# Two matmul stages in a fixed order: the second stage of batch 0 moved ahead of batch 1's products

## What is computed

```python
x = x + matmul(fake_quant(layernorm(x)), fake_quant(ctx))       # per batch
x = x + ffn(layernorm(x))
# fake_quant(v) = (clip(round(v / s + z), 0, 255) - z) * s
# ffn(y): logits = y @ W_router.T                               # 8 experts
#         combine = top 2 of softmax(logits), renormalised
#         h = (y @ A_e.T) * combine_e                           # rank 16 each
#         out = y @ W_base.T + b_base + 2.0 * sum_e(h_e @ B_e.T)
```

## Time and profile before

| | before |
|---|---|
| median of the runs | 189.27 us |
| span of the profiled execution | 187.8 us |
| TensorE (PE) busy | 164.8 us, 88% |
| VectorE (DVE) busy | 127.8 us, 68% |
| ScalarE (ACT) busy | 75.0 us, 40% |
| GpSimd (POOL) busy | 37.8 us, 20% |
| HBM read, written | 18.38 MB, 4.19 MB |

### The profile page before, as it was taken

How to read it: one execution, slowest core, us unless ns; L and a number is a source line. 1 busy time by engine, 2 the same in 40 slices (tenths; PEclk the granted TensorE clock), 3 DMA queues, 4 the chain that set the end, 5 groups by cost and what they waited for, 6 DMA issues and landing times.

```text
span 187.8 us, 2573 instructions
## 1 busy us (share of the span) xinstructions
PE 164.8 (88%) x946; PEld 88.2 (47%) x946; DVE 127.8 (68%) x284; ACT 75.0 (40%) x100; POOL 37.8 (20%) x110
## 2 busy tenths in 40 slices
PE   6639997894697969369999999999999999999992
PEld 3323443351263427126556556556556556556541
DVE  6996577899666995995872872872882882831821
ACT  3476393997285923545124124124124124120000
POOL 8804504045500000080031031031021021000000
PEclk9975999999789999999999999999999999999999
DMA  5999999999300000000200200200200200200211
GB/s 116 401 417 410 409 408 407 409 409 411 127 5 0 0 0 0 0 0 3 112 2 3 112 0 0 112 3 0 112 0 3 112 0 0 108 7 0 105 65 56
DMA packets 6780, 22.74 MB, mean 121 GB/s; under 512 B 880, under 2 KB 1136, under 8 KB 6768
## 3 DMA queue, kind: packets, MB, share of 16 engines
q1 hardware_dynamic: 6624, 22.58, 30.8%
q10 hardware_dynamic: 144, 0.00, 0.0%
HBM read 18.38 MB, written 4.19 MB: 120 GB/s over the span
## 4 chain that ended last, share of the span: by engine, by line
PE 66%; DVE 28%; issue 3%; POOL 1%; DVEq 0%; POOLq 0%
PE ps L753 39%; PE ps L713 8%; PE ps L743 6%; DVE w_lo L522 4%; PE ps L722 3%; DVE xs L468 3%; PE ps L735 2%; PE ps L734 2%; PE ps L736 2%; DVE a L595 2%; DVE xs L417 2%; DVE a L454 2%; DVE bnx L427 2%; DVE bnx L425 2%; DVE a_t L461 1%
## 5 line engine op out<-in xcount | busy, mean ns | idle before, releaser
L753 PE MATMUL ps<-w_hi,yt_hi 128*128 128x512 f16 x128 | 39.5, 380 | 6.0 <-DVE w_lo L522 6.0
L713 PE MATMUL ps<-a,a_t 128*128 128x512 f16 x128 | 34.6, 407 | 6.9 <-DVE a_t L461 6.8
L753 PE MATMUL ps<-w_hi,yt_lo 128*128 128x512 f16 x128 | 39.4, 379 | 0.0
L753 PE MATMUL ps<-w_lo,yt_hi 128*128 128x512 f16 x128 | 39.4, 379 | 0.0
L287 ACT ACTIVATE a<-stage,prm,inv_s 128x1024 uint8<-128x1024 f32 x16 | 19.6, 1240 | 12.0 <-DMA stage<-in_ctx_kv 11.7
L713 PEld LDWEIGHTS ps<-a,a_t 128*128 128x128 f16 x128 | 12.4, 103 | 23.6 <-DVE a_t L461 10.2
L550 DVE MAX8 top<-ps 128x8 f32<-128x8 f32 x8 | 1.4, 175 | 30.6 <-PE ps L736 30.6
L235 POOL TENSOR_SCALAR root<-mvy 128x1 f32<-128x1 f32 (+1 forms) x7 | 2.9, 413 | 87.9 <-DVE mvy L421 87.9
L337 ACT ACTIVATE y<-xs,y_bias,y_scale 128x1024 f32<-128x1024 f32 x8 | 9.9, 1239 | 26.5 <-POOL y_bias L258 26.4
L753 PEld LDWEIGHTS ps<-w_hi,yt_hi 128*128 128x128 f16 x128 | 11.4, 98 | 18.3 <-DVE w_lo L522 7.7
L753 PEld LDWEIGHTS ps<-w_hi,yt_lo 128*128 128x128 f16 x128 | 12.5, 98 | 15.1
(11 more groups left out here) (127 smaller groups left out, 266.7 us busy)
## 6 DMA issues: line engine op xcount, KB each, us to landing
stage<-in_ctx_kv SPq DMA_DIRECT2D x16, 512.0 KB, 13.5
stage<-in_w_t SPq DMA_DIRECT2D x8, 512.0 KB, 11.8
xs<-in_x SPq DMA_DIRECT2D x7, 512.0 KB, 13.5
out_dram<-xs SPq DMA_DIRECT2D x7, 512.0 KB, 2.7
ar_raw<-in_ar_t SPq DMA_DIRECT2D x1, 544.0 KB, 15.9
xs<-in_x SPq DMA_DIRECT2D x2, 256.0 KB, 3.7
b_raw<-in_b_t SPq DMA_DIRECT2D x1, 512.0 KB, 11.2
bias_sb<-in_bias SPq DMA_DIRECT2D x1, 512.0 KB, 12.0
```

The costliest lines, as they stand in the source:

```text
L713: last = nc.tensor.matmul(ps[:, s1_bank(t) + h, :], a1_t[:, t % 4, k, :], a2[:, n, h * H:(h + 1) * H], start=k == 0, stop=k == K - 1)
L753: ins = nc.tensor.matmul(ps[:, OUT_BANK[p] + h, :], part, rhs[:, k, h * H:(h + 1) * H], start=k == 0 and part is hi and rhs is w_hi, stop= ...
```

## The change

Line numbers in `order` rows are those of the kernel that the rows are of.

- **SyncE** loads ar and w straight behind batch 0's context, then tile 4 of x, b, the bias and the other x tiles. Batch 1's context comes last and takes over the slots of w, so each of its tiles waits for a w_lo.
- **TensorE** runs the first stage of tiles 0 to 3 alone. Then come the wide products of tiles 0 and 1 in two passes: the parts hi x hi and lo x hi (which need only w_hi) first, w_lo's part later, with narrow, lora and the column sums of batch 1 in between. The products of tiles 4 to 7 stand inside the wide products of tiles 2 to 5. Two to five extra matmuls on constants (keep_warm, ten in all) stand between the first column sums.
- **ScalarE** reads the peaks of w two tiles at a time, splits w earlier and quantises batch 1's context after that. It no longer makes y for tiles 0 and 1.
- **GpSimd** makes y for tiles 0 and 1 (one instruction of 128x1024 each, the new make_y). scale_x and scale_y run for one tile at a time from tile 4 on and alternate.
- **VectorE** has one common scale chain for w and ar instead of two. The column term is a function of its own (add_corr) before statistics_y, on VectorE for all tiles as before, and so is the bias. The cast of the identity (ident16) stands earlier. From tile 2 on the work of three tiles is interleaved.
- The PSUM banks are dealt out anew: batch 1's products use the banks of y's transposes (6 and 7), so make_corr(1) must have read the column sums before them, and sum_x1 must have read each product before the next transpose of y.

```diff
@@ SyncE
+            def load_ctx(n):
+                if n >= K:
+                    sp.wait_ge(w_lo_ready, n - K + 1)
+                sp.dma_start(stage[:, n % RING, :], ctx_tiles[n]).then_inc(stage_in[n % RING], 16)
+            def load_w(k):
+                sp.wait_ge(ctx_ready, k + 1)
+                sp.dma_start(stage[:, k, :], w_tiles[k]).then_inc(stage_in[k], 16)
...
@@ GpSimd
+            def make_y(t):
+                pool.wait_ge(y_scaled, t + 1)
+                if t > 0:
+                    pool.wait_ge(y_transposed, t)
+                nc.gpsimd.tensor_scalar(y[:, :], xs[:, t, :], y_scale[:, t:t + 1], y_bias[:, t:t + 1], ALU.mult,
+                                        ALU.add).then_inc(y_ready, 1)
...
             scale_x(2, 4)
-            scale_x(4, 6)
-            scale_x(6, 8)
-            scale_y(0, 2)
-            for t in range(2, T):
-                scale_y(t, t + 1)
+            scale_y(0)
+            make_y(0)
+            scale_y(1)
+            make_y(1)
+            scale_y(2)
+            scale_x(4, 5)
+            scale_y(3)
+            for t in range(2, T - 1):
+                if t >= 3:
+                    scale_y(t + 1)
+                if t + 3 < T:
+                    scale_x(t + 3, t + 4)
@@ ScalarE
+            peaks_ar()
             act.wait_ge(consts_ready, 2)
             make_corr(0)
+            for i in range(K // 2):
+                peak_of_two_w(i)
+            split_first_yt()
+            for k in range(K):
+                split_w(k)
+            split_yt(1)
+            split_ar()
+            split_b()
+            for n in range(K, K + 6):
                 quantise_ctx(n)
...
@@ VectorE
             take_a1t(3)
+            sum_x1(2)
+            spread_peaks()
+            make_scales()
+            split_first_yt()
+            add_corr(1)
+            statistics_y(1)
+            sum_x1(3)
+            for k in range(4):
+                split_w(k)
+            split_yt(1)
+            split_ar()
+            for k in range(4, K):
+                split_w(k)
+            add_corr(2)
+            statistics_y(2)
+            gate_tile(0)
+            split_b()
+            statistics_x(4)
+            split_hct(0)
+            add_corr(3)
+            statistics_y(3)
+            gate_tile(1)
             quantise_x(4)
+            split_yt(2)
...
+            for t in range(2, T):
                 gate_tile(t)
+                if t + 2 < T:
+                    take_a1t(t + 2)
                 sum_out(t - 1)
...
@@ TensorE
+            def late_product(t):
+                pe.wait_ge(a1t_ready, t + 1)
+                pe.wait_ge(corr_ready, 2)
+                for k in range(K):
+                    product(t, k)
...
+            for k in range(K):
+                pe.wait_ge(w_hi_ready, k + 1)
...
+                wide(0, k, False, parts=(0, 2))
+            transpose_y(1)
+            pe.wait_ge(x1_summed, TB)
+            pe.wait_ge(yt_lo_ready, 2)
+            for k in range(K):
+                wide(1, k, False, parts=(0, 2))
...
+            transpose_hc(1)
+            pe.wait_ge(yt_lo_ready, 3)
+            for k in range(K):
+                column_sums(1, k)
+            lora(1, stop=True)
+
+            for t in range(2, T - 1):
                 pe.wait_ge(yt_lo_ready, t + 1)
                 narrow(t)
...
                 for k in range(K):
                     wide(t, k, k == K - 1)
+                    if k == 0 and t + 2 < T:
+                        transpose_a1(t + 2)
+                    if k == 2 and t + 2 < T:
+                        late_product(t + 2)
```

More of the change, by code:

```diff
@@ L41, in xattn_ffn @@
     WARM_UP = 24
+    KEEP_WARM = (2, 5, 3)
     RING = 8
@@ L472, in sum_x1 @@
                     op0=ALU.mult, op1=ALU.add).then_inc(x1_summed, 1)
-            def spread(peaks, i):
-                return nc.vector.tensor_scalar(diag[:, i, :], ident16[:, :], peaks, None, ALU.mult)
-            def to_powers(first, last):
-                some = slice(first, last)
-                then(nc.vector.tensor_scalar(power[:, some], power[:, some], FLOOR, None, ALU.max))
-                then(nc.vector.tensor_scalar(power[:, some].bitcast(I32), power[:, some].bitcast(I32), EXPONENT, None,
-                                             ALU.bitwise_and))
-                then(nc.vector.reciprocal(scale[:, some], power[:, some]))
@@ L499, in split_ar @@
+                then(nc.vector.tensor_scalar(den_scale, power[:, 2:3], ratio, None, ALU.mult))
             def split_ar():
@@ L625, in _ @@
             take_a1t(2)
+            add_corr(0)
+            statistics_y(0)
             quantise_x(3)
[L627 to L628 removed]
             sum_x1(1)
             take_a1t(3)
[L631 to L641 removed]
@@ L670, in _ @@
+            add_corr(2)
[3 more added lines that the diff above has]
+            statistics_x(4)
+            split_hct(0)
+            add_corr(3)
+            statistics_y(3)
+            gate_tile(1)
+            quantise_x(4)
+            split_yt(2)
+            split_hct(1)
             add_bias(0)
-            for t in range(1, T):
+            sum_out(0)
+            add_bias(1)
+            for t in range(2, T):
                 gate_tile(t)
+                if t + 2 < T:
+                    take_a1t(t + 2)
@@ L691, in _, with keep_warm @@
         def _(pe):
+            def keep_warm(n):
+                for _ in range(n):
+                    nc.tensor.matmul(ps[:, WARM_BANK, 0:3 * P], ones16[:, 0:P], ones16[:, :], start=True, stop=True)
             def transpose_a1(t):
                 pe.wait_ge(x_quantised, t + 1)
-                if t >= 2:
-                    pe.wait_ge(a1t_ready, t - 1)
+                if t == TB:
+                    pe.wait_ge(x1_summed, TB)
+                elif t >= 2:
+                    pe.wait_ge(a1t_ready, t - 1 if t < TB else t)
                 bank = ps[:, a1_bank(t), :].bitcast(F16)
@@ L746, in lora, with wide @@
                     ins.then_inc(out_done, 1)
-            def wide(t, k, stop, halves=range(NH)):
+            def wide(t, k, stop, halves=range(NH), parts=(0, 1, 2)):
                 p = t % 2
                 hi, lo = yt_hi[:, p, k, :], yt_lo[:, p, k, :]
-                for part, rhs in ((hi, w_hi), (hi, w_lo), (lo, w_hi)):
+                every = ((hi, w_hi), (hi, w_lo), (lo, w_hi))
+                for i in parts:
+                    part, rhs = every[i]
                     for h in halves:
                         ins = nc.tensor.matmul(ps[:, OUT_BANK[p] + h, :], part, rhs[:, k, h * H:(h + 1) * H],
-                                               start=k == 0 and part is hi and rhs is w_hi, stop=stop and part is lo)
+                                               start=k == 0 and i == 0, stop=stop and i == 2)
                 if stop:
@@ L765, in _ @@
             column_sums(0, 2)
-            for t in range(T):
+            keep_warm(KEEP_WARM[2])
+            for t in range(TB):
                 pe.wait_ge(a1t_ready, t + 1)
@@ L806, in _ @@
+            pe.wait_ge(x1_summed, TB)
+            pe.wait_ge(yt_lo_ready, 2)
+            for k in range(K):
+                wide(1, k, False, parts=(0, 2))
+            pe.wait_ge(ar_lo_ready, 2)
+            narrow(0)
+            for k in range(K):
+                pe.wait_ge(w_lo_ready, k + 1)
+                wide(0, k, False, parts=(1,))
+            narrow(1)
+            transpose_hc(0)
+            for k in range(K):
+                wide(1, k, False, parts=(1,))
                 if k == 4:
-                    transpose_y(1)
+                    pe.wait_ge(b_lo_ready, 1)
+                    lora(0, stop=True)
```

306 lines of the change are left out of this document (114 added, 192 removed).

## The result

The kernel after takes 188.34 us (median of 20 runs, 186.70 to 189.22), the kernel before 189.26 us in runs taken beside it: a ratio of 0.993, 95% interval 0.991 to 0.996. So it is faster, by 0.9 us in place of the forecast 5.2 us, and its time lies 0.6 us above the upper end of the range. The profiled execution has a span of 186.5 us where 182.7 us were forecast. The runs of after fall in two groups: eight with a mean granted clock near 0.98 take 186.7 to 187.4 us, twelve with 0.963 to 0.972 take 188.1 to 189.2 us. The profiled one is of the larger group. The smaller group lies inside the forecast's range; the larger one, and with it the median, does not.

What follows compares the result with a forecast made beforehand. TensorE's gapless end was taken as the bound, preceded by 13.8 us of waits to win. Start 74.4, gapless work 104.6, stall 0.35 and tail 3.3 gave a 182.7 us span, 184.1 us as timed; range 180.9 to 187.7 us.

Steps and rivals of the forecast that it cites:

- The block: Gapless TensorE work from batch 1's column sums on: 104.6 us, plus 0.35 us of stall.
- the tail behind it: From TensorE's last work to the end of the span: 3.3 us, untouched by the change.
- 0.35 us of stall in the first tile: First tile with a product laid in: VectorE's work up to take_a1t exceeds TensorE's 7.2 us by 0.35 us.
- Step 1, loads: Loads of ar and w behind batch 0's context, 4.75 MB at 409 GB/s: 11.6 us, w's last tile lands at 31.5 us.
- Step 2, the peaks: Scale of w: peaks read and spread, then TensorE's peak matmul, two product steps and y(0)'s transposes, done at 36.4 us.
- T: Start of batch 1's column sums, where TensorE's gapless work begins: 74.4 us.
- Steps 3 and 4: w_hi on ScalarE from 37.5 us; GpSimd's scale chain 6.9 us, y(1) 1.7 us; VectorE has y(1) split at 53.1 us.
- Step 5, VectorE decides: From y(1)'s split to batch 1's column sums VectorE works without a gap, 21.3 us; TensorE needs 19.2 us.
- TensorE's lower clock in the new gaps: Rival: half clock for some 5 us behind the new waits; 185.5 to 187.7 us, most likely 186.4; chance 0.17.
- The 1.47 us: Added to the profiled span to get the time of the runs: median 189.27 us against a span of 187.8 us.
- VectorE as the bound of the block: Rival: GpSimd's two scale chains per tile slow VectorE's gate; about 190 us, slower than before; chance 0.06.
- GpSimd not held up: Rival: GpSimd's chain for y(1) runs in 3.0 us, column sums start 2.9 us sooner; 181.2 us; chance 0.14.

Runs made afterwards that it cites:

- fill_peaks: Kernel after with 15 extra 128x384 matmuls on constants in TensorE's wait for the peaks of w: median 186.94 us, ratio 0.987.
- fill_all: Kernel after with such matmuls in four waits: peaks of w (15), around y(1)'s transposes (12, 14), before batch 1's column sums (9): median 185.11 us, ratio 0.977.
- fill_y1: Kernel after with 12 and 14 extra matmuls on constants in the two waits around y(1)'s transposes: median 186.43 us, ratio 0.979.
- before_fill: Kernel before with ten extra matmuls between the first column sums and 22 in the 3.87 us wait before tile 5's product: median 187.50 us, ratio 0.990.
- before_fill_all: Kernel before with before_fill's extra matmuls plus 4, 6, 10 and 13 in tile 0's waits for w_lo: median 187.29 us, ratio 0.988.
- clean_chain: Kernel after with VectorE waiting for y(1) before its first w_lo, statistics_x(4) moved into that wait: median 185.31 us, ratio 0.974.
- fill_both: Kernel after with extra matmuls in the wait for the peaks (15) and around y(1)'s transposes (12, 14): median 186.61 us, ratio 0.982.
- clean_fill_all: clean_chain with extra matmuls at the peaks (15), behind y(1)'s transposes (14) and at the column sums (9): median 183.11 us, ratio 0.967.

## Why the prediction was wrong

- **The block.** Right: 104.84 us measured, 104.95 us forecast; the tail behind it 3.2 us, forecast 3.3. Laying batch 1's products into the wide products cost TensorE just their own time. A little luck is in it: of the 0.35 us of stall in the first tile only some 0.1 us came (its a_t is ready at 89.03 us, the product starts at 89.09 us), and small terms made up the rest.
- **Step 1, loads.** The last w tile was read from 32.35 us, forecast 31.5: 0.85 us. Holding back the other loads did not help, so the estimate from 4.75 MB at the mean rate was too short by itself; why is open.
- **Step 2, the peaks.** This is where the clock first counts. The forecast's prices for what stands behind the wait (0.86 us of products, 0.87 us of transposes) are those of a full clock. Their rows read 1.52 and 1.91 us, against 1.03 and 1.04 us in fill_peaks, where the clock is full: 1.2 us of T.
- **Steps 3 and 4.** w_hi started at 39.62 us, forecast 37.5 (steps 1 and 2 together). The chain for y(1) took 6.5 us, forecast 6.9, held up as the earlier trace rows said; make_y took 1.20 us where 1.7 us was taken between 0.9 and 2.3. Together they give 0.9 us back. At a full clock (fill_all) VectorE ends split_yt(1) at 53.67 us, forecast 53.1; in after at 54.7 us.
- **Step 5, VectorE decides.** Right as a sum: in fill_all 21.2 us from there to T, forecast 21.3. Wrong in after, where it took 23.7 us. The 2 us of slack that TensorE was given (19.2 against 21.3 us) held only at a full clock: tile 1's first parts took 2.5 us more, and VectorE waited 2.03 us for narrow(0). fill_y1 took this wait away.
- **The step that failed** is the price of TensorE's work behind the new waits. Steps 2 and 5 put all of it at the full clock's 0.2156 us a matmul and the lower clock at nothing; in after two matmuls behind y(1)'s split take 1.01 to 1.06 us in place of 0.59, and the lower clock cost 3.4 us of span (after against fill_all). In the forecast's own terms it was the choice among the cases: TensorE's lower clock in the new gaps stood as a rival with 0.17, and it was what happened, by the mechanism and at the places that it named. Its most likely time, 186.4 us, assumed one part of the costs; its upper end, 187.7 us, took the costs on tile 1's parts and on tile 3's last steps together, 3.6 us, and both came, 3.4 us. The other 0.8 us are small: 0.4 us of the way to T at a full clock (183.1 in place of 182.7 us of span), and 0.4 us more outside the span (188.34 - 186.5 = 1.84 in place of 1.47 us): 184.1 + 3.4 + 0.4 + 0.4 = 188.3 us. The 1.47 us came from a median less the span of another execution: in the runs of before that have both figures it is 1.8 us too (189.28 us with a span of 187.5 us).
- **Why 0.17 was too little.** The argument against it was that the waits of up to 2.4 us near 80 us "left no mark". before_fill shows the flaw: in its profiled execution that same wait of 2.38 us is followed by a dip, and in its other five runs the mean clock of 1.00 leaves no room for one. A wait without a mark in one trace was no evidence that such a wait is always free.
- **What the gain was made of.** 5.1 us of span were forecast as the gain of the order. 2.3 us of it were the clock loss of the kernel before, which the forecast let vanish and the new waits brought back, larger. The order itself is worth 2.4 us between the spans of before_fill_all and fill_all, 2.0 to 2.2 us by their runs.
- **The other rivals.** VectorE as the bound of the block: no; between 97.00 and 115.00 us it is busy 13.06 of 18.00 us and TensorE all of them. GpSimd not held up: not in after; clean_chain had to make it so.

The row of that last reading, from the stretches of after:

```profile
97.00:115.00 18.00, 18.00 (x112) 10.22 (x111) 13.06 (x27) 3.80 (x7) 4.46 (x18) 1.00 0.08 30
```

## What to carry to other kernels

Before the gain of a new order is added up, find out what the granted clock takes from both orders: a kernel's own dips are in its time and are easily counted as waits that the new order removes. Where a change opens several waits of 1.5 to 3 us on TensorE, count on the lower clock behind some of them, price the work behind each at half clock, and see which engine is waiting for just that work; dummies on constants in all of the waits are a cheap remedy, in some of them alone the dip may only move, as it did here. A chain of small GpSimd steps on the path is best given a stretch in which VectorE does not read two SBUF operands, even if VectorE has to wait for it.

## What the runs showed that was not expected

- With some waits filled, the clock fell behind another that had shown nothing, though not in every execution: the column sums (1.53 us of wait, 3.63 us in after, 5.31 us in fill_both and clean_chain) and the wait for w_lo in before_fill. The length of a wait alone does not tell: 2.46 us before y(1)'s products was followed by a dip in after, 2.56 us at the same place in clean_chain, where the wait of 2.15 us ahead of it is gone, was not. What tells them apart was not settled.
- The dips also go with the spread of the times: fill_all and clean_fill_all have all runs within 0.8 us, the kernel after within 2.5 us.
- One GpSimd instruction of 128x1024 with one SBUF input and two scalars takes 1.20 us, ScalarE's same work 1.24 us.
